# One spline stage, three edits: six result buffers with x accumulated ahead, the linear part on GpSimd, and the far cubic part added in PSUM by a float32 product with the identity

## The reference, cut to what matters

```python
out = relu(batchnorm(conv3x3(x, sign(w1))))
out = batchnorm(conv3x3(out, sign(w2)))
x = relu(out + x)
# the spline
x_aff = clip(x * a[c] + b[c], -1.5, 1.5)
u = (x_aff + 1.0) * 0.5 * (K - 1);  i = floor(u);  t = u - i
spline = alpha_table[i0]*b0(t) + alpha_table[i1]*b1(t) + alpha_table[i2]*b2(t) + alpha_table[i3]*b3(t)
y_nl = einsum('bchwr,cr->bchw', spline, mix)
return id_gain[c] * x + y_nl + bias[c]
```

## Time and profile before

| | before |
|---|---|
| median of 3 runs | 1254.49 us (1253.94 to 1254.75) |
| the profiled execution | 1254.66 us, span 1252.8 us |
| VectorE busy | 1062.8 us, 85% of the span |
| TensorE busy | 1058.6 us, 85% |
| ScalarE busy | 868.8 us, 69% |
| GpSimd busy | 113.4 us, 9% |

### The profile page before, as it was taken

How to read it: one execution, slowest core, us unless ns; L and a number is a source line. 1 busy time by engine, 2 the same in 40 slices (tenths; PEclk the granted TensorE clock), 3 DMA queues, 4 the chain that set the end, 5 groups by cost and what they waited for, 6 DMA issues and landing times. The chain is left out here.

```text
span 1252.8 us, 51454 instructions
## 1 busy us (share of the span) xinstructions
PE 1058.6 (85%) x23562; PEld 710.2 (57%) x23562; DVE 1062.8 (85%) x951; ACT 868.8 (69%) x424; POOL 113.4 (9%) x189
## 2 busy tenths in 40 slices
PE   6999996999999368887888788878887888788876
PEld 4688885788888234554545455444544545455444
DVE  5765656766666689999999999999999999999987
ACT  4454544777787267688868877887788778877881
POOL 6000000282000000000000000000000000000000
PEclk9999998999999778998989889898998989889898
DMA  7666766576777386677767766777677667776552
GB/s 227 259 257 256 276 255 225 217 277 252 271 264 300 136 235 181 183 216 194 185 189 213 196 181 193 208 192 184 189 214 192 184 197 206 194 182 197 157 114 78
DMA packets 58215, 260.85 MB, mean 208 GB/s; under 512 B 16336, under 2 KB 16336, under 8 KB 50000
## 3 DMA queue, kind: packets, MB, share of 16 engines
q1 hardware_dynamic: 52528, 230.88, 56.3%
q0 software_dynamic: 4608, 25.69, 11.0%
q10 hardware_dynamic: 928, 1.90, 0.6%
HBM read 104.29 MB, written 77.07 MB: 145 GB/s over the span
## 5 line engine op out<-in xcount | busy, mean ns | idle before, releaser
L1181 PE MATMUL tab<-edge_mask,diag 128*32 128x392 bf16 x10240 | 501.8, 358 | 132.6 <-DVE poly L1090 130.8
L1181 PEld LDWEIGHTS tab<-edge_mask,diag 128*32 128x32 f16 x10240 | 281.7, 104 | 339.0 <-DVE poly L1090 143.4
L982 ACT ACTIVATE edge_mask<-cell,thr 128x6272 bf16<-128x6272 bf16 x62 | 338.5, 5508 | 0.0
L711 PE MATMUL acc<-split,w 64*64 64x392 f16 x4608 | 195.9, 329 | 12.0 <-DVE w L463 10.8
L711 PE MATMUL acc<-band_split,w 64*64 64x392 f16 x4608 | 197.9, 330 | 9.4 <-ACT band_split L368 7.2
L410 ACT ACTIVATE yout<-acc 128x1568 f32<-128x1568 f32 x64 | 94.2, 1473 | 160.6 <-PE acc L711 139.4
L1181 PE MATMUL tab<-middle_mask,diag 128*32 128x392 bf16 x4096 | 183.4, 332 | 25.0 <-DVE middle_mask L1052 25.0
L711 PEld LDWEIGHTS acc<-band_split,w 64*64 64x64 f16 x4608 | 164.1, 107 | 42.9 <-issue 14.1
L711 PEld LDWEIGHTS acc<-split,w 64*64 64x64 f16 x4608 | 155.3, 107 | 51.9 <-issue 12.6
L520 DVE BATCH_NORM_STATS2 stats<-yout 128x392 f32 (+1 forms) x240 | 118.0, 555 | 60.2 <-ACT yout L410 59.4
L930 ACT ACTIVATE zbuf<-lin,cst 128x1568 f32<-128x1568 f32 x32 | 54.3, 1697 | 163.8 <-DVE lin L1016 157.9
(11 more groups left out here) (126 smaller groups left out, 816.9 us busy)
## 6 DMA issues: line engine op xcount, KB each, us to landing
y_scratch<-yout SPq DMA_DIRECT2D x32, 1568.0 KB, 6.2
cell<-cell SPq DMA_DIRECT2D x496, 98.0 KB, 3.3
xin<-y_scratch SPq DMA_DIRECT2D x16, 1568.0 KB, 9.0
zbuf<-y_scratch SPq DMA_DIRECT2D x32, 784.0 KB, 5.9
lin<-in_x SPq DMA_DIRECT2D x32, 784.0 KB, 6.1
lin<-far POOLq DMA_DIRECT2D x32, 784.0 KB, 8.8
out<-lin SPq DMA_DIRECT2D x31, 784.0 KB, 4.1
xin<-in_x SPq DMA_DIRECT2D x15, 1568.0 KB, 9.3
```

The lines of the kernel that those rows point to most:

```text
L711: mm = pe.matmul(acc[h * C:(h + 1) * C, 2 * k + r, 0:TILE], weights[part][own, tap * C:(tap + 1) * C], image[own, first:first + ROWS, dx:d ...
L982: act.activation(mask_of(b, q)[:, :, :], cell4[b % 2][:, :, :], ACT.Sign, bias=thr[:, q:q + 1]).then_inc(sign_mask_ready, 1)
L1181: mm = pe.matmul(tab[(b + t) % 2][j * GROUP:(j + 1) * GROUP, sub, 0:SUB], keep["diag"][part][:, j % 2, t, q, :], mask_of(b, q)[:, j, sub * ...
```

## The change

- **x is accumulated ahead.** y is loaded into one of now six `lin` buffers (SyncE, for c+4). ScalarE scales it in place (`scale`, new). A GpSimd-issued DMA then adds x from HBM onto it (`add_x`). This replaces VectorE's `total` from chunk 2 on. `position` of c+2 reads the sum.
- **The linear part goes to GpSimd** (`linear`, one operation on 128 x 1568 float32), in front of the `add_x` of the next chunk.
- **The far part is added by TensorE.** `far_part` becomes a plain product, and after the masks of VAL four float32 products of `far` with a 128 x 128 identity (`add_far`, 392 columns each) add it into the same PSUM table. The DMA that did it (L919) goes.
- **The polynomial is evaluated with two products by the offset** in place of the squared distance. ScalarE's `distance_square` and the tensor `dist_sq` go; VectorE has the same number of operations for it.
- **Orders.** VectorE's `fixed` of c+2 stands in front of `near_cube` of c, and `finish` of c-1 behind it. ScalarE's `far_distance` of c waits for VAL of c-1. SyncE stores c-1 behind the copies of c+2.
- **Small ones.** The wait for the stores of y2 moves from the end of the convolutions to the load of chunk 2. ScalarE's first operation is a square root. The loops over four chunks are written out in full.

```diff
@@ spline, ScalarE
+            def scale(c):
+                act.wait_ge(y_loaded[c % LIN], 16 * (c // LIN + 1))
+                act.activation(lin_of(c)[:, :], lin_of(c)[:, :], ACT.Identity, scale=cc(BN2_S)).then_inc(scaled, 1)
...
+                    act.wait_ge(x_added, 16 * (c - 1))
...
-                wait_past(act, far_added, 16 * c)
+                wait_past(act, table_ready, TABLES * c)
@@ spline, GpSimd
-                pool.wait_ge(far_part_ready, 2 * c + 2)
-                pool.dma_start(lin[c % BUFS][:, :], far[:, :], accum_op=ALU.add).then_inc(far_added, 16)
+                pool.wait_ge(place_ready, c + 1)
+                pool.tensor_scalar(lin_of(c)[:, :], lin_of(c)[:, :], cc(NEG_B2),
+                                   par[:, ID_GAIN:ID_GAIN + 1], ALU.max, ALU.mult).then_inc(lin_ready, 1)
...
+                pool.wait_ge(scaled, c - 1)
+                pool.dma_start(lin_of(c)[:, :], image_half(x, c), accum_op=ALU.add).then_inc(x_added, 16)
@@ spline, VectorE
-                dve.scalar_tensor_tensor(out=far[:, :], in0=far[:, :], scalar=cc(AMP), in1=far_sq[:, :],
-                                         op0=ALU.mult, op1=ALU.mult).then_inc(far_part_ready, 2)
+                dve.tensor_tensor(far[:, :], far[:, :], far_sq[:, :], ALU.mult).then_inc(far_part_ready, 1)
...
+            def times_offset(c, t, done):
+                dve.wait_ge(table_used, used(c, t))
+                dve.scalar_tensor_tensor(out=poly[c % 2][:, :], in0=offset[c % 2][:, :], scalar=1 / POINT,
+                                         in1=poly[c % 2][:, :], op0=ALU.mult, op1=ALU.mult).then_inc(done, 1)
@@ spline, TensorE
+            def add_far(c, sub):
+                return pe.matmul(tab[(c + T_VAL) % 2][:, sub, 0:SUB], keep["ident"][:, :],
+                                 far[:, sub * SUB:(sub + 1) * SUB], start=False, stop=True)
...
+                if t == T_VAL:
+                    pe.wait_ge(far_part_ready, c + 1)
+                    for sub in range(4):
+                        mm = add_far(c, sub)
                 mm.then_inc(table_ready, 1)
```

More of the change, by code:

```diff
@@ L134, in convolutions @@
         loaded = [sem(f"x_loaded{b}") for b in range(2)]
-        stored = [sem(f"y_stored{b}") for b in range(2)]
+        stored = keep["y_stored"]
         early_loaded = sem("early_x_loaded")
@@ L824, in quarters, with summed @@
             return t[:, :].rearrange("p (q x) -> p q x", q=4)
[L826 to L844, removed]
+        def summed(c, t):
+            return tab[(c + t) % 2][:, :, 0:SUB]
@@ new lines, in store @@
+            def store(c):
+                sp.wait_ge(whole, c + 1)
+                sp.dma_start(image_half(out, c), lin_of(c)[:, :]).then_inc(stored[c % LIN], 16)
+            spread(0)
+            for b in range(2):
+                sp.wait_ge(keep["y_stored"][b], 16 * PAIRS)
+            load(2)
+            spread(1)
+            load(3)
+            for c in range(CHUNKS):
+                if c + 4 < CHUNKS:
+                    load(c + 4)
+                if c + 2 < CHUNKS:
+                    spread(c + 2)
+                if c > 0:
+                    store(c - 1)
@@ L1008, in _, with edge @@
-            rounds(act, body)
+            def edge(c, q):
+                act.wait_ge(copied[c % 2], 256 * (c // 2 + 1))
+                wait_past(act, table_ready, TABLES * (c - 1))
+                act.activation(mask_of(c, q)[:, :, :], cell4[c % 2][:, :, :], ACT.Sign,
+                               bias=thr[:, q:q + 1]).then_inc(sign_mask_ready, 1)
+            for c in range(2):
+                position(c)
+                cells(c)
+                spread(c)
+            distance(0)
+            scale(2)
@@ L1070, in far_cube, with base, near_cube @@
-            def far_cube(i, b):
-                c = BUFS * i + b
+            def base(c, t):
+                return (keep["plain"] if c == 0 else first)[:, t:t + 1]
+            def near_cube(c):
+                dve.wait_ge(far_ready, c + 1)
+                dve.wait_ge(table_ready, used(c, T_NEAR))
+                dve.scalar_tensor_tensor(out=quarters(poly[c % 2]), in0=summed(c, T_NEAR), scalar=base(c, T_NEAR),
+                                         in1=quarters(poly[c % 2]), op0=ALU.add, op1=ALU.mult).then_inc(table_used, 1)
@@ L1172, in _ @@
-            rounds(dve, body)
+                    dve.wait_ge(table_used, used(c, T_VAL) + sub)
+                    dve.scalar_tensor_tensor(out=lin_of(c)[:, own], in0=poly[c % 2][:, own], scalar=cc(AMP),
+                                             in1=lin_of(c)[:, own], op0=ALU.mult, op1=ALU.add).then_inc(whole, 1)
+            total(0)
+            total(1)
+            for c in range(2):
+                fixed(c)
+                offsets(c)
+            first_masks()
+            for c in range(CHUNKS):
+                if c > 0:
+                    add_table(c - 1, T_VAL, slope_ready, c)
+                if c + 2 < CHUNKS:
+                    fixed(c + 2)
+                near_cube(c)
+                if c > 0:
+                    finish(c - 1)
+                far_cube(c)
+                far_part(c)
+                if c + 1 < CHUNKS:
+                    for q in MIDDLE_QUADS:
+                        middle(c + 1, q)
+                add_table(c, T_SQ, table_used, used(c, T_NEAR))
+                times_offset(c, T_SQ, near_ready)
+                add_table(c, T_LIN, near_ready, c + 1)
+                times_offset(c, T_LIN, slope_ready)
+                if c + 2 < CHUNKS:
+                    offsets(c + 2)
```

351 lines of the change are left out of this document (126 added, 225 removed).

## The result

| | before | after |
|---|---|---|
| median | 1254.61 us (1253.94 to 1254.75, 4 runs) | 1327.64 us (1324.08 to 1328.63, 4 runs) |
| ratio | | 1.0578 [1.0557, 1.0599] |
| profiled execution | 1254.66 us | 1328.63 us |
| VAL of chunk 0 to VAL of chunk 30 | 750.06 us | 813.85 us |

What follows compares the result with a forecast made beforehand. The prediction took a 24.39 us chain through TensorE and VectorE, 27.04 with the products, to bound the kernel. 1254.66 + 61.1 (steady part) + 2.65 (tail) + 5.9 (start) = 1324.3 us; 8-in-10 range 1268 to 1372.

Steps and rivals of the forecast that it cites:

- the 24.39 us chunk near the end: Chunks 29 to 30, with no chunk left to prepare: VectorE's work falls to 20.69 us, the chunk still takes 24.39.
- the chain: Steps from VAL to the next VAL, each released by the one before: 24.39 us, forecast 27.04 with the float32 products.
- The price of the products: Four float32 products between VAL's masks and NEAR: 2.65 us a chunk, bounds 1.33 and 5.3.
- the masks 4.45 for 4.35: First link, VAL's 64 mask products on TensorE: claimed to stay at 4.35 us.
- far_cube to VAL: Last link, from far_cube through two middle masks and the adding of SQ to the next VAL: 9.13 us.
- the steady part: The 30 chunks from VAL of chunk 0 to VAL of chunk 30: 811.2 against 750.06 us, +61.1.
- The two-round rival: Float32 products in TensorE cost only two rounds, 1.33 us a chunk: 1283 us in total, chance 0.13.
- The tail: VAL of chunk 30 adds its own float32 products after the steady chunks: +2.65 us.
- The start: Start of the spline stage: far_cube of chunk 0 waits behind chunk 2's accumulated x, +5.9 us, with -3 included.
- The clock: TensorE's granted clock falls to 0.50 behind the idle time of about 3.95 us in front of VAL.
- its rival: TensorE's clock no longer falls at VAL: masks 2.65 us, chain 25.34, total 1273 us; chance 0.12 with a dear product.
- The rival with GpSimd in front: GpSimd's `linear` goes before VectorE's `fixed` and blocks it: far_cube 2.2 us late, chain 29.2, 1390 us; chance 0.10.

Runs made afterwards that it cites:

- the single-edit run: The changed kernel with only the linear part moved back from GpSimd to VectorE, float32 products kept: 1325.34 us.

## Why the prediction was right

- **The bound.** The forecast took the 24.39 us chunk near the end, not VectorE's nearly full queue, as what decides. The far part alone on the kernel before (27.16 us a chunk, though VectorE's work stayed at 24.5) and the masks moved out of the chain (22.9) both show it.
- **The price of the products**, taken as 2.65 us between 1.33 and 5.3, measured 2.83. 30 chunks at 0.18 more are 5.4 us, the largest error of the sum. Every other link went the other way or held: the masks 4.45 for 4.35 in the ordinary chunk but 2.8 in one, far_cube to VAL 9.02 for 9.13, so that the steady part is +63.8 for +61.1. The two-round rival is refuted. What carried the choice was that each of the two records moves twice the bytes; the sign that the forecast gave for it, records of 0.33 us, came as records of 0.49 us whose starts lie 0.35 us apart.
- **The tail**: from VAL of chunk 30 to the end of the span 36.84 us after, against 34.16 before (1252.80 - 1218.64): +2.68 for +2.65.
- **The start**: VAL of chunk 0 is 7.5 us later for +5.9. 1.4 us of this lies ahead of the stage; the rest, 6.1, is as forecast, though not quite by its parts: the first `total` gained 2.1 us instead of 3, counted from the end of the convolutions, the accumulated x of chunk 2 landed some 9.5 us behind `scale` and not 8.8, and GpSimd's hold on `offsets` was not foreseen. That `distance` of chunk 0 still began where forecast (449.66, 448.3 without the 1.4) is luck: its own copies held ScalarE for 5.96 us there and not for 7.12. (The forecast's 462.2 + 1.1 + 1.85 is 465.15, not 465.3, which changes nothing here.) Together: 63.8 + 2.7 + 7.5 = 74.0, from 1254.66 to 1328.63.
- **The clock** fell as forecast, but the profile holds its rival as well: in one chunk it did not, which took 25.53 us (forecast 25.34), with the same 3.83 us of idle time in front. Why it did not fall there is open.
- **The waits.** The forecast saw waits of VectorE in front of near_cube and far_cube (1.12 and 0.75 us) and none of note elsewhere; in the ordinary chunk it also waits 0.89 us for the VAL table and 1.36 us for `position` in front of `fixed`. Neither reaches the chain.
- **GpSimd** is where the reasoning was weakest. The upper bound for its operation, 4.5 us from one with fewer columns, was too low: 5.6 alone. The forecast said the operation ends before far_cube and costs nothing; it ends 1.0 us before (731.20 + 6.44 against 738.64), having stretched `finish` to 2.79. That stretch is also most of why VectorE is busy 84% of the chunk and not 80 (0.95 of 1.4 us). The conclusion held for the steady chunks, as the single-edit run shows (27.22 us either way). It hung on who comes first: VectorE by 0.08 us in the chunk shown, and all 32 `fixed` operations take 1.10 us, so it was first in the others as well. The rival with GpSimd in front is real, and appears as soon as VAL comes earlier.
- **Not foreseen**: that the gains of single repairs would not add up. Taking 2.83 us out of the chain let GpSimd in; taking 2.06 out let the clock take half of it back in every second chunk.

## What to carry to other kernels

When two engines hand a double buffer back and forth, their nearly full queues may hide a loop through both that is as long. Look for a place where one of them has less to do (the last iterations, here) and see whether the period falls with it. Work added inside that loop costs in full, work removed beside it gives nothing; first ask which operation in the loop could stand elsewhere, here two masks of together 3.6 us, and only then take work off. Before an operation goes to GpSimd, find which VectorE operation is released by the same event, and who comes first.

## What the runs showed of the hardware

- A float32 product of 128x128 weights and 392 columns leaves two matmul records of 492 ns each, but eight of them start within 2.83 us, so one product costs 0.71 us; in float16 it is one record and 0.19 us, 3.7 times less. The Trainium skill (FP8 and Floating Point Precision, TensorE Precision Notes) gives four passes for true FP32. The trace agrees in the price, 3.7 times that of float16, but shows two records a product, so it can't tell four passes from two slower ones; the number of records alone would have misled.
- GpSimd's operation with two constants on 128x1568 float32 takes 5.62 us by itself, the same on VectorE 1.09. VectorE's one-input operations (`fixed`, `offsets`) and GpSimd's exclude each other: 6.14 us for VectorE's 1.10 behind GpSimd, 6.44 for GpSimd's 5.62 behind VectorE. The Trainium skill (SBUF — State Buffer, "SBUF: two separate sides") calls it an exclusive lock that whoever starts first keeps for the whole instruction, and for these the trace agrees. It names VectorE operations with two SBUF inputs as well, and there the trace differs: `finish`, which has two, starts at 735.11 while GpSimd's runs to 737.64, and ends at 737.90 after 2.79 us instead of 1.84, so it is slowed and not held. An operation that reads PSUM and one SBUF tensor keeps its 1.85 us. Released together, VectorE was first by some 0.07 us.
- The granted clock fell behind 3.83 us of idle time in all the 30 chunks but one. What one repair gives back therefore depends on the period that it leads to: with the float16 product VAL's record alternated between 4.44 and 5.42 us. With 0.31 us of idle time in front of VAL the clock stayed at 2.4 GHz from 500 to 1100 us (masks out of the chain), and so it did with several gaps a chunk of 0.4 to 1.2 us (the same order with the linear part on GpSimd, 1.00 from 500 to 1150 us).
